# Attention and mixture of experts on one core: queries and keys projected already transposed, and routing moved later

## The reference

```python
xn = _layernorm(x)                                    # no weights
q, k, v = split(xn @ Wqkv.T)                          # 16 heads of 8
q = q * cos + _rotate_half(q) * sin                   # pairs (2i, 2i+1) turned by position
k = k * cos + _rotate_half(k) * sin
scores = q @ k.T / sqrt(8)                            # only j <= i and i - j <= 64
y = softmax(scores) @ v
attn = y @ Wproj.T + bproj

gates = xn @ gate_w.T + gate_b                        # 8 experts
weights, indices = top_k(gates, 2); weights = softmax(weights)
for e in range(8):
    h = gelu(xn @ w1[e] + b1[e])                      # 128 -> 512
    out += w_e * (h @ w2[e] + b2[e])                  # 512 -> 128
result = x + attn + out
```

## Time and profile before

| | us |
|---|---|
| median of 3 runs | 709.84 (705.51 to 714.12) |
| profiled execution | 706.8 |
| its span | 705.0 |

### The profile page before, as it was taken

One profiled execution on the slowest core, in us unless ns is written; L12 is line 12 of the kernel. 1 busy time (PEld: TensorE's weight loads), 2 busy tenths in 40 slices (PEclk: granted clock), 3 DMA queues, 4 the chain that ended last, 5 costly groups with the idle time before them and its releaser, 6 DMA issues.

```text
span 705.0 us, 26353 instructions
## 1 busy us (share of the span) xinstructions
PE 634.6 (90%) x10179; PEld 512.1 (73%) x10179; DVE 474.0 (67%) x1312; ACT 359.4 (51%) x683; POOL 382.8 (54%) x489
## 2 busy tenths in 40 slices
PE   5667889988689989999999899999999999999884
PEld 2545567766466667767777899999999999996653
DVE  7878878888788868888886444545454444446764
ACT  1343656655356656666666344444444444446561
POOL 1775877666355646656630454545454545453443
PEclk9797989999999999999999999999999999999996
DMA  9686965985868868787877888787777777774988
GB/s 270 190 212 168 252 178 157 261 238 167 245 187 236 220 200 228 200 220 213 219 200 230 252 237 243 227 248 238 234 236 238 228 234 238 243 237 134 309 260 233
DMA packets 156236, 157.92 MB, mean 224 GB/s; under 512 B 20225, under 2 KB 131097, under 8 KB 156113
## 3 DMA queue, kind: packets, MB, share of 16 engines
q1 hardware_dynamic: 141576, 135.29, 67.2%
q0 software_dynamic: 8416, 17.51, 7.3%
q10 hardware_dynamic: 6120, 3.43, 1.8%
HBM read 102.19 MB, written 58.61 MB: 228 GB/s over the span
## 4 chain that ended last, share of the span: by engine, by line
PE 67%; DVE 12%; DMA 7%; issue 6%; SPq 4%; POOL 3%; ACT 1%; ACTq 0%; DVEq 0%; POOLq 0%
PE ps L791 16%; PE ps L778 15%; PE ps L726 7%; PE ps L661 4%; DVE mx L1040 4%; PE ps L634 4%; PE ps L668 3%; PE ps L710 3%; PE ps L754 2%; DMA xn<-slots_x 2%; PE ps L764 2%; PE ps L703 2%; PE ps L645 2%; PE ps L699 2%; PE ps L739 2%
## 5 line engine op out<-in xcount | busy, mean ns | idle before, releaser
L1338 POOL DMA_INDIRECT chosen_y<-xn,to x135 | 129.6, 960 | 133.6 <-DVE xn L1102 111.7
L1040 DVE TENSOR_REDUCE mx<-ps 128x8 f32<-128x1024 f32 x128 | 156.4, 1222 | 57.9 <-PE ps L668 57.8
L1236 ACT ACTIVATE hb<-ps,xn 128x256 f32<-128x256 f32 x284 | 113.2, 461 | 140.9 <-PE ps L778 140.9
L1332 POOL DMA_INDIRECT slots_x<-xn,pos x128 | 131.5, 1027 | 93.7 <-PE ps L710 73.8
L1214 ACT ACTIVATE PT<-ps 128x1024 f32<-128x1024 f32 x128 | 131.1, 1024 | 79.7 <-PE ps L710 79.4
L791 PEld LDWEIGHTS ps<-xn,hb 128*128 128x128 f32 x1080 | 131.1, 192 | 3.5 <-ACT hb L1236 0.2
L791 PE MATMUL ps<-xn,hb 128*128 128x128 f32 x1080 | 132.1, 275 | 0.0
L778 PE MATMUL ps<-xn 128*128 128x256 f32 (+1 forms) x568 | 128.5, 369 | 0.0
L778 PEld LDWEIGHTS ps<-xn 128*128 128x128 f32 x568 | 99.1, 190 | 9.9
L726 PE MATMUL ps<-PT,V 128*32 128x64 f32 (+1 forms) x3072 | 85.8, 245 | 1.2 <-ACT Os L1221 0.6
L1096 DVE TENSOR_TENSOR xn<-ps,xn 128x256 f32<-128x256 f32 x71 | 29.1, 410 | 77.1 <-PE ps L791 77.0
(11 more groups left out here) (149 smaller groups left out, 887.8 us busy)
## 6 DMA issues: line engine op xcount, KB each, us to landing
xn<-experts SPq DMA_DIRECT2D x71, 578.0 KB, 4.0
QK<-stack SPq DMA_DIRECT2D x128, 192.0 KB
stack<-sp SPq DMA_DIRECT2D x64, 192.0 KB
xn<-slots_x SPq DMA_DIRECT2D x64, 132.0 KB
stack<-sp SPq DMA_DIRECT2D x64, 128.0 KB
xn<-chosen_y SPq DMA_DIRECT2D x32, 256.0 KB, 4.6
stack<-sp SPq DMA_DIRECT2D x64, 64.0 KB
Vc<-values SPq DMA_DIRECT2D x32, 128.0 KB
```

The costliest lines, as they stand in the source:

```text
L1040: e.tensor_reduce(mo[:, :, :, c, t], ps[:, 0:2, :].rearrange("p g (h k) -> p g h k", k=P), AX.X, ALU.max, negate=True).then_inc(v_mx, 1)
L1236: e.activation(hb[:, s, c, 0:m], ps[:, 2 * s + c // 2, (c % 2) * SL:(c % 2) * SL + m], ACT.Gelu, bias=b1b[:, i % NW, c:c + 1]).then_inc(a_ ...
L1332: e.indirect_dma_start(out=Xs, out_offset=bass.IndirectOffsetOnAxis(ap=pos[:, n, u:u + 1], axis=0), in_=xn[:, u, :], in_offset=None).then_ ...
L1338: e.indirect_dma_start(out=Ys, out_offset=bass.IndirectOffsetOnAxis(ap=to[:, i % 4, j:j + 1], axis=0), in_=yb[:, i % 4, j, :], in_offset=N ...
```

## The change

1. The weights of queries and keys are held with even and odd dimensions apart, in an order made by one copy on POOL, and are what TensorE loads; xnT is what it streams. The product comes out with the dimensions in the partitions (queries in the upper 64, keys in the lower 64) and even and odd in the two halves of the columns. The rotation becomes one multiplication and one with the halves exchanged. `turn_qk`, `rc` and the semaphore `e_qt` are gone.
2. `rest` now reads both its inputs from SBUF, `hi` writes its part twice, so that each side of the stack is a range of `sp`, and the twelve planes are written in four DMAs. `load` takes its 48 rows as twelve planes of four rows.
3. `turn` and `vg` use bank 6 alone, `qk`, `turn_m` and `count` bank 5 alone, and an odd unit's `down` bank 6.
4. FIRST goes from -22 to -20. `qk` moves from the third quarter of four to the first, `rope` to the second, `add` and `hi` to the fourth, `rest`, `mid` and `lo` to the first of the next four. `mput` stands first in its quarter. `vload` is a quarter earlier relative to its use.
5. Routing begins in quarters 4, 12 and 20. The scatters begin at q = 12, one a quarter until q = 22 and then on average 1.55 a quarter, for 1.29 before. The parts of `table` are four quarters apart, from q = 31, for one quarter apart from q = 30. `clear_ends` goes from quarter 27 to 29.

```diff
-FIRST = -22
+FIRST = -20
 def routed(k):
-    return FIRST + 4 * ((BT.index(RT[k + 1]) - 2) // 2)
+    return FIRST + 24 + 8 * k
-SPREAD = (1.05, 1.05, 2.0, 1.05)
+SPREAD = (2.0, 1.1, 1.0, 2.1)
...
-    first = ((), (), (), (("yT", -7),))
-    middle = ((("add", 20), ("out", -4), ("mput", 4), ("residual", -8)), (("hi", 19),),
-              (("norm_y", -6), ("rest", 18), ("mget", 2), ("expand", 2)), (("rope", 21), ("mid", 17)))
-    late = ((("turn_qk", 20), ("lo", 16), ("write", 16)), (("turn_o", -5), ("msplit", 7), ("write", 15)),
-            (("qk", 22), ("turn_y", -6)), (("lo", 17), ("vload", 5), ("load", 13), ("proj", -7), ("turn_m", 5)))
+    first = ((("mput", 4),), (), (), (("yT", -7),))
+    middle = ((("rest", 16), ("out", -4), ("residual", -8), ("mid", 16)), (("rope", 19),),
+              (("norm_y", -6), ("mget", 2), ("expand", 2)), (("add", 17), ("hi", 17)))
+    late = ((("qk", 20), ("lo", 16)), (("turn_o", -5), ("msplit", 7), ("write", 15)),
+            (("turn_y", -6), ("vload", 6)), (("load", 13), ("proj", -7), ("turn_m", 5)))
...
-        if ROUTE + 12 <= q < ROUTE + 21:
-            order.append(("table", q - ROUTE - 12))
+        if ROUTE + 11 <= q < ROUTE + 47 and (q - ROUTE - 11) % 4 == 0:
+            order.append(("table", (q - ROUTE - 11) // 4))
...
-        due += SPREAD[q % 4] if q >= routed(0) + 8 else 0
+        due += (SPREAD[q % 4] if q >= ROUTE + 2 else 1.0) if q >= routed(0) + 8 else 0
...
-    Dst = [nc.dram_tensor(f"stack_{i}", (2, 6, P, 256), bf16).ap() for i in range(3)]
+    Dst = [nc.dram_tensor(f"stack_{i}", (6, 2, P, 256), bf16).ap() for i in range(3)]
-        sp = sb("sp", [P, 2, 2, 3, 256], bf16)
+        sp = sb("sp", [P, 2, 4, 512], bf16)
...
         def bank(n):
-            return (7, 4)[n] if n < 2 else 6 - n % 2
+            return (7, 4)[n] if n < 2 else 6
...
                 elif what == "write":
-                    for d0, n in ((0, 3), (3, 2), (5, 1)):
-                        e.dma_start(Dv[0, :, d0:d0 + n, :], sp[:, s, 0, 0:n, :]).then_inc(d_w[b % 3], 16)
-                    for d0, n, s0 in ((0, 3, 0), (3, 2, 1), (5, 1, 2)):
-                        e.dma_start(Dv[1, :, d0:d0 + n, :], sp[:, s, 1, s0:s0 + 1, :].broadcast_to(
-                            (P, n, 256))).then_inc(d_w[b % 3], 16)
+                    for r, d0, n0, n in ((slice(0, P), 0, 2, 4), (slice(0, 64), 4, 0, 8), (slice(64, P), 4, 4, 4),
+                                         (slice(64, P), 8, 0, 4)):
+                        e.dma_start(D[r, d0:d0 + n, :], own[r, n0:n0 + n, :]).then_inc(d_w[b % 3], 16)
                 elif what == "load":
                     for i in range(2):
-                        Dv = Dst[b % 3][i].rearrange("s (d h) t -> (s d) (h t)", h=16)
+                        Dv = Dst[b % 3].rearrange("s o (a d h) t -> a (s o) d (h t)", a=2, h=16)[i]
                         for g in range(2):
                             e.dma_start(QK[64 * g:64 * g + 48, s, i, :],
-                                        Dv[:, g * 2048:(g + 1) * 2048]).then_inc(d_r[s], 16)
+                                        Dv[:, :, g * 2048:(g + 1) * 2048]).then_inc(d_r[s], 16)
...
-                    for t in range(2):
-                        c0 = (2 * b + t) * P
-                        k = e.matmul(ps[:, 5, t * 256:(t + 1) * 256], xnT[:, c0:c0 + P], wq_s[:, 0:256], start=True,
-                                     stop=True, skip_group_check=True)
+                    c0 = 2 * b * P
+                    for o in range(2):
+                        k = e.matmul(ps[:, 5, o * 256:(o + 1) * 256], wq_s[:, o, :, :].rearrange("p n h -> p (n h)"),
+                                     xnT[:, c0:c0 + 256], start=True, stop=True, skip_group_check=True)
-                elif what == "turn_qk":
-                    e.wait_ge(v_rc, b + 1)
-                    for t in range(2):
-                        for i in range(2):
-                            k = e.transpose(ps[:, 6, i * 256 + t * P:i * 256 + (t + 1) * P],
-                                            rc[:, t * 256 + i * P:t * 256 + (i + 1) * P], identf)
...
                     if b:
-                        e.wait_ge(v_rc, b)
+                        e.wait_ge(a_hi, b)
+                        e.wait_ge(v_rr, b)
...
-                    e.tensor_tensor(rc[:], ra[:], rb[:], ALU.add).then_inc(v_rc, 1)
+                    e.tensor_tensor(ra[:], ra[:], rb[:], ALU.add).then_inc(v_rc, 1)
...
-                    e.tensor_tensor(rr[:, b % 2, :].rearrange("p (a t) -> p a t", a=2),
-                                    ps[:, 6, :].rearrange("p (a t) -> p a t", a=2), sp[:, b % 2, :, 0, :],
-                                    ALU.subtract).then_inc(v_rr, 1)
+                    e.tensor_tensor(rr[:, b % 2, :], ra[:], sp[:, b % 2, 2, :], ALU.subtract).then_inc(v_rr, 1)
...
-                    e.activation(sp[:, b % 2, :, 0, :], ps[:, 6, :].rearrange("p (a t) -> p a t", a=2),
-                                 ACT.Copy).then_inc(a_hi, 1)
+                    e.activation(sp[:, b % 2, 2:4, :], ra[:].unsqueeze(1).broadcast_to((P, 2, 512)), ACT.Copy).then_inc(a_hi, 1)
```

More of the change, by code:

```diff
@@ L176, in schedule @@
                 order.append(("count", k))
-        put(late, q)
         maxima(q)
@@ L369, in attention_moe_kernel @@
         d_o, d_one = semaphore("d_o"), semaphore("d_one")
-        e_xt, e_vg, e_rt, e_qk, e_qt, e_sc, e_mt, e_st = (semaphore("e_" + n) for n in (
-            "xt", "values", "route", "qk", "qkT", "scores", "maxT", "scoresT"))
+        e_xt, e_vg, e_rt, e_qk, e_sc, e_mt, e_st = (semaphore("e_" + n) for n in (
+            "xt", "values", "route", "qk", "scores", "maxT", "scoresT"))
         e_pv, e_ot, e_yt, e_pr, e_xs, e_up, e_dn = (semaphore("e_" + n) for n in (
```

82 lines of the change are left out of this document (34 added, 48 removed).

## The result

The changed kernel takes **725.96 us** (median of 4 runs, 719.77 to 727.39); the kernel before, run beside it, 711.98 (705.51 to 714.83). The ratio is 1.018, 95% interval 1.013 to 1.023: slower, by more than the 1% that a measurement here can tell. The forecast was 692, range 677 to 712.

The account below looks back on a forecast made before the run. TensorE was taken to bound most of the kernel (67% of the chain), VectorE the head, and waits quarters 32 to 55. 706.8 - 6.5 - 4.0 - 5.5 = 690.8, named as a median of 692 us, range 677 to 712.

Parts of the forecast that it names:

- quarters 32 to 103: Steady stretch: 18 batches lose 0.59 us of TensorE transposes each, half kept against later loads; -5.5 us.
- rival C: Load as 12 planes of 4 rows uses fewer DMA engines and takes longer; slower, 725 to 739 us; chance 0.10.
- The late path: Quarters 32 to 103: writes land 0.7 to 1.7 us later against the load; priced at half of TensorE's 0.6 a batch.
- Four DMAs for six, at 0.5 each, give 1.0 back of the issuing: Writes to the stack on SP's queue: fewer DMAs shorten issuing by 1.0 us, though not the landing.
- Head, -6.5: Before the first scores: 3.5 us from two quarters fewer, 3.0 (half of 6.0) from routing's first piece leaving.
- Quarters 0 to 31, -4.0: After the head: transposes -4.7, waits -2.5, projections moved in +1.4, routing moved in +1.8 us.
- The clears, 0: Eight clears block SP's queue 9.02 us; a load wait of the same size stays, 0, ends -5 and +4.
- Transposes, 0.59 a batch: Four `turn_qk` transposes go, so TensorE gets back 0.59 us a batch.
- Experts and end, 0: Last stages: only a bank's number changes and the last six batches have no `turn_qk`; 0, ends -1 and +2.
- A: Whole kernel: everything comes through, loads have slack and the clears' wait shrinks; about 682 us; chance 0.25.
- B: Late path turns TensorE's 0.6 a batch into load waits of `scores`, head keeps half; 702 us; chance 0.16.
- D: Head keeps its 72.4 us and routing's arrival eats quarters 0 to 31; 706 to 709 us; chance 0.04.

Follow-up runs that it names:

- e2: The kernel before with only its load read as 12 groups of 4 rows instead of 48 rows: 729.64 us, ratio 1.018.
- the square: Four kernels with full-width writes; all writes behind `lo`, or its plane alone: load in 12 groups 1.029, 1.001; as 48 rows 1.001, 0.983 (repeat 0.982).
- e8: The changed kernel with a seven-plane stack, writes over all 128 partitions, projection columns reordered and the load as 48 rows again: 714.85 us, ratio 1.001.
- e10: e8 with only `lo`'s plane written behind `lo`, the other four writes right behind `mid`: 700.73 us, ratio 0.983.

## Why the prediction was wrong

The sign and the range failed. The waits that decided were named in the text, but as rivals with 0.16 and 0.10, and not in the sum. The step that failed is the one on quarters 32 to 103, "I take half, 0.3: 18 x 0.3 = 5.4": these quarters were to gain 5.5 us and lost 16.0 (+6.9, +9.1). It has two wrong terms.

- **The load's own form was put at nothing, and left to rival C (0.10).** It costs 1.8% in the kernel before (e2) and 1.8 to 2.8% in the square, that is 13 to 20 us. The page of the Trainium skill that spoke for it was named beside C, and was set aside because no row of before shows such a load. But the trace of before did show that there was no room for one: three of four loads already waited for their writes, and the scores already waited for theirs (the 2.0 us in 4 waits above).
- **The late path was capped at TensorE's gain.** That writes land "0.7 to 1.7 us later against the load" was right: against the fourth exponential they complete 1.3 us later (2.1 us behind it for 0.8, in the table of the chain). But its price was taken as at most the 0.6 us a batch that TensorE wins, and half of it. A late chain is not capped by what was won. e8, the changed kernel without the load's form, stands at 1.001 where the forecast is 0.977, so something still eats the rest of the gain: the late path, and the transposes' smaller gain (below). With the planes of `mid` and `hi` written ahead (e10) 1.8%, some 13 us, come back. What the 1.1 us of `lo` cost by themselves no run isolates.
- **That C's 725 to 739 holds the measured 726 is in part luck.** C has +29 to +43 us in quarters 32 to 103 and -10.5 in the stages before; measured are +16.0 and -3.9. Its load is 1.5 to 2.3 us longer; measured are 0.6. The two errors cancel in the total.
- **"Four DMAs for six, at 0.5 each, give 1.0 back of the issuing"** was wrong: four take 2.6 to 3.9 us where six took 3.0 to 4.5, and the 3.0 of the earlier trace rows is the shortest of them. The medians in 262 to 385 us are 3.3 and 3.6, so 0.3 came back. e8 shows why a price per DMA misleads.
- **Head, -6.5.** It came as -0.5, since the same late load held the scores for 8.1 us. With the chain shortened (e10) exponential 0 is at 66.07, 7.0 ahead of before and where "near 66" was forecast. That supports the reading of the work on norm, routing and transposes, but not each of its terms: "half, 3.0" was a guess, and e10 still waits 2.7 us for loads there.
- **Quarters 0 to 31, -4.0:** -3.4. Right in sum; its parts were not measured one by one, but for `rest`. The Trainium skill's rule against it (SBUF — State Buffer, on the shared port pair) would have cost 5 us. They did not come: `rest` took 680 to 922 ns there with a median of 682, and the addition, 674 to 1960 in the earlier trace rows, took 679 to 684. The rows of the changed kernel:

```profile
L1015 DVE TENSOR_TENSOR rr<-ra,sp x8: 680/682/922, 82.5 to 175.8; 128x512 f32<-128x512 f32 x8
```

```profile
L1008 DVE TENSOR_TENSOR ra<-ra,rb x8: 679/681/684, 79.8 to 173.7; 128x512 f32<-128x512 f32 x8
```

The rule agrees with the trace of before; what failed were the 5 us worked out from it, which took for granted that `rest` would meet such an operation. Every addition there that took over 0.75 us (six of 32) overlaps `lo` on GpSimd, and each ends 0.55 us after `lo` does. One of them:

```profile
167.47 1.18 POOL L1278 TENSOR_TENSOR sp<-rr,sp 128x512 bf16<-128x512 f32 x1
...
167.89 1.32 DVE L1024 TENSOR_TENSOR rc<-ra,rb 128x512 f32<-128x512 f32 x1
```

In the changed kernel `lo` waits for `mid` and so for `rest`, and the addition stands in another quarter: none of the 64 additions and `rest`s overlaps `lo`. 38 of them overlap scatters and take 0.68 to 0.75 us, but for the one of 0.92.

- **The clears, 0.** The queue was blocked as long as before (8.78 us), but what stood behind it was a load that had no slack and took 3.35 us to issue: 10.68 us of idle TensorE for 4.52, and an interval of 13.9 us for 9.1: +4.8. "A wait of the same size stays" was the error; the ends (-5, +4) fell just short of it.
- **Transposes, 0.59 a batch.** Where nothing is late (e10), a steady batch takes 9.80 us for 9.94. The windows of these two batches, e10's first, say where the rest went:

```profile
305.61:315.41 9.80, 9.57 (x259) 6.73 (x262) 8.68 (x14) 7.00 (x10) 7.30 (x7) 1.00 0.84 239
```

```profile
265.16:275.10 9.94, 9.94 (x263) 7.22 (x265) 8.53 (x14) 6.66 (x10) 6.33 (x6) 1.00 0.83 227
```

  TensorE's busy time falls by 0.37 us with the four transposes, not by the 0.59 between two starts, and 0.23 of that comes back as idle time, most of it before `turn_y`, which waits for VectorE's `norm_y` (2.5 us in 8 waits, 262 to 385). So 0.14 of 0.59 arrives. Over quarters 56 to 103 it is 0.9 us for 7.1, but there the two traces compare less well: the profiled run of before, 706.8 us, is among its fastest.
- **Experts and end, 0:** -0.5 and +1.4.
- **Small slips.** A's own terms add up to 679.7 or less and not 682, and half of B and D make 0.12 within 1% and not 0.14. Neither bears on the outcome.

What stays open: the experts' stage of the profiled runs moved between 259 and 265 us from kernel to kernel without an edit there; why the writes' total issue stays near 3 to 4 us however they are cut was not settled, only that they need not all stand behind `lo`; nor what decides the gain of spread clears.

## What to carry to other kernels

Before counting what an edit takes off the busiest engine, follow the chain that feeds it and ask for its slack. Here SP's short waits for the writes, with the scores' short waits for the load, already said that there was none, and what is added to such a chain comes out as waits of the busiest engine: in many batches, in the head, and again behind each blocked queue. A DMA rewritten with fewer instructions is not a cheaper DMA: look at its dimensions and at how its rows divide, and change them alone in the old kernel, which here would have shown the loss. What needs a value last should wait for it alone: one plane's write behind `lo`, with the rest sent ahead, was worth about as much as the load's form (1.8% each, where the other was mended).
